# Turning the third batch's probabilities with VectorE and DRAM transfers in a fused cross-attention, convolution and expert kernel

## The reference, cut to what matters

```python
# x (128, 32, 1024), ctx (128, 257, 256); 32 heads of 32, 8 key groups, 4 heads each
scores = einsum('bsgrd,btgd->bgrst', layernorm(x), ctx) / sqrt(32) + mask
x = x + einsum('bgrst,btgd->bsgrd', softmax(scores), ctx)      # cross-attention
x = x + (fft-convolution of layernorm(x) with an S4 kernel + D*u)
z = layernorm(x) @ A.T                                         # 64 experts, rank 8
x = x + ((z * gate) @ B.T) * 2.0                               # gate: softmax over top 16
```

## Time and profile before

| | |
|---|---|
| median of 3 runs | 1288.2 us (1287.83 to 1289.85) |
| the profiled execution | 1290.52 us, span 1288.6 us, mean granted clock 0.992 |
| PE busy | 1232.9 us, 96% of the span |
| ACT, DVE, POOL busy | 1122.9, 959.7, 825.4 us |
| DMA | 166.38 MB, mean 129 GB/s |

### The profile page before, as it was taken

The page is one execution under the profiler, slowest core; times in us unless marked ns, Lnnn a source line. Parts: engine busy times, 40 slices in busy tenths (PEclk is TensorE's granted clock), DMA queues, the critical chain, the costliest instruction groups (busy, mean ns, idle before and its releaser), DMA issues.

```text
span 1288.6 us, 41515 instructions
## 1 busy us (share of the span) xinstructions
PE 1232.9 (96%) x13676; PEld 1083.1 (84%) x13676; DVE 959.7 (74%) x3424; ACT 1122.9 (87%) x3337; POOL 825.4 (64%) x1259
## 2 busy tenths in 40 slices
PE   3679999999999999999999999999999999999997
PEld 2558888888888888888888888888888888888886
DVE  6977777777777777877777777677777877877753
ACT  5889999998999999999999999989999999999841
POOL 4447676776667677666767766676777666777520
PEclk9979999999999999999999999999999999999999
DMA  7443443443344444434544433453443344444210
GB/s 237 134 127 93 151 155 122 130 133 125 119 148 152 124 130 132 129 123 141 155 122 131 147 124 118 134 154 123 131 151 123 122 128 154 132 125 132 61 60 33
DMA packets 150103, 166.38 MB, mean 129 GB/s; under 512 B 58217, under 2 KB 116082, under 8 KB 149890
## 3 DMA queue, kind: packets, MB, share of 16 engines
q1 hardware_dynamic: 149890, 163.72, 40.9%
HBM read 128.50 MB, written 34.08 MB: 126 GB/s over the span
## 4 chain that ended last, share of the span: by engine, by line
PE 76%; DVE 5%; DMA 4%; POOL 4%; ACT 4%; issue 3%; SPq 2%; DVEq 0%; ACTq 0%; POOLq 0%
PE ps_p L562 22%; PE ps_p L633 15%; PE ps_p L661 12%; PE ps_p L648 12%; PE ps_p L594 8%; PE ps_s L574 7%; ACT pr L840 2%; DMA dn<-den 2%; DMA xq<-in_x 1%; POOL lastp L1093 1%; DVE ms L1387 1%; SPq L381 1%; ACT pts L772 1%; DMA vl<-in_ctx 1%; POOL lastp L1103 1%
## 5 line engine op out<-in xcount | busy, mean ns | idle before, releaser
L840 ACT ACTIVATE pr<-ms,negmax 128x256 f32<-128x256 f32 x1024 | 512.6, 504 | 17.3 <-DVE negmax L1387 17.3
L1387 DVE CUSTOM_DVE_ANT_0 ms<-ps_s,neg_mask,last 128x256 f32<-128x256 f32 x1024 | 447.0, 473 | 7.1 <-PE ps_s L574 6.2
L772 ACT ACTIVATE pts<-ps_p 128x512 f32<-128x512 f32 x512 | 298.3, 590 | 45.8 <-PE ps_p L562 29.1
L562 PE MATMUL ps_p<-ident,pr 128*128 128x128 f32 x2048 | 296.5, 280 | 10.4 <-ACT pr L840 5.1
L562 PEld LDWEIGHTS ps_p<-ident,pr 128*128 128x128 f32 x2048 | 229.1, 142 | 48.0 <-issue 17.4
L840 ACT ACTIVATION_READ_ACCUMULATOR pr<-ms,negmax 128x1 f32 x1024 | 199.6, 195 | 0.0
L1061 POOL TENSOR_TENSOR kt<-kr,kt 128x512 fp32r<-128x512 f32 x128 | 164.9, 1288 | 24.1 <-ACT kt L772 24.1
L648 PE MATMUL ps_p<-wa_hi,ut_hi 128*128 128x288 f32 x512 | 159.6, 312 | 1.4 <-DVE ut_lo L1203 1.4
L648 PE MATMUL ps_p<-wa_lo,ut_hi 128*128 128x288 f32 x512 | 151.8, 296 | 0.0
L648 PE MATMUL ps_p<-wa_hi,ut_lo 128*128 128x288 f32 x512 | 151.7, 296 | 0.0
L1203 DVE TENSOR_TENSOR ut_lo<-ps_p,ut_hi 128x512 fp32r<-128x512 f32 x128 | 87.7, 690 | 74.8 <-ACT ut_hi L772 74.5
(11 more groups left out here) (139 smaller groups left out, 2584.6 us busy)
## 6 DMA issues: line engine op xcount, KB each, us to landing
cx<-in_ctx SPq DMA_DIRECT2D x128, 256.0 KB, 3.9
kr<-in_keys SPq DMA_DIRECT2D x128, 256.0 KB, 3.0
xq<-in_x SPq DMA_DIRECT2D x32, 512.0 KB, 4.3
turn_q<-xq SPq DMA_DIRECT2D x32, 512.0 KB, 2.9
qx<-turn_q SPq DMA_DIRECT2D x128, 128.0 KB, 2.9
xr<-in_x SPq DMA_DIRECT2D x32, 512.0 KB, 3.9
out_x<-tmp SPq DMA_DIRECT2D x32, 512.0 KB, 3.2
dn<-den SPq DMA_DIRECT2D x512, 2.0 KB, 2.3
```

The lines of the kernel that those rows point to most:

```text
L562: mm = pe.transpose(into[:, j * P:(j + 1) * P], source, ident[:, :])
L772: return act.activation(out, in_, ACT.Copy, scale=scale)
L840: act.activation(pr[:, b % 2, g, :], ms[:, n % MS, :], ACT.Exp, bias=negmax[:, n % MS:n % MS + 1], scale=-1.0, accum_out=den[:, b, g:g + 1 ...
L1387: dve.tensor_tensor_reduce(ms[:, n % MS, :], ps_s[:, g % GPH, g // GPH * SW:(g // GPH + 1) * SW], neg_mask[:, 0:SW], 1.0, last[:, it % 2, ...
```

## The change

`TURNED = (2,)`: batch 2 of every tile no longer has pair chunks 8 to 11 on PE nor their copies on ACT. Instead
- `exp` writes its 8 groups with the 256 keys split in 2 x 4 x 32, so that in each half (4 groups) a run of 128 elements holds 32 keys of four groups;
- `p_turn` (DVE) transposes the 32x32 blocks of a half in place, 128x1024, twice per tile;
- `store_p` (SP) writes a half, 512 KB, to the DRAM tensor `turn_p`, twice per tile;
- `load_p` (SP) reads it back with keys on the partitions: four transfers of 256 KB into the half of `pts` that batches 0 and 2 share. It waits for both stores and for attend 1;
- `attend` 4 and 5 wait for these four transfers and read `pts` with a view whose runs are 32 elements long.

`move_q` now makes four transfers of 128 partitions each, one per batch, and `load_last` one transfer instead of four. `exp` waits per half of `pr`. `PAIRS` becomes 12. All `BANKS` numbers and all lists of calls are new. Cut to its core:

```diff
+TURNED = (2,)
+def paired(m):
+    return sum(k // GPH not in TURNED for k in range(m))
+PAIRS = paired(STEPS // 2)
+        turn_p = nc.dram_tensor("turn_p", [len(TURNED), P, GPH, HALVES, SW], F32, kind="Internal").ap()
+            def store_p(it, k, h):
+                sp.wait_ge(p_turned[k][h], at(it, 1, 1))
+                if at(it, 64, 0) > 0:
+                    sp.wait_ge(p_loaded[k], at(it, 64, 0))
+                sp.dma_start(turn_p[k, :, :, h, :],
+                             pr[:, TURNED[k] % 2, GPH * h:GPH * (h + 1), :]).then_inc(p_stored[k][h], 16)
+            def load_p(it, k):
+                b = TURNED[k]
+                for h in range(HALVES):
+                    sp.wait_ge(p_stored[k][h], at(it, 16, 16))
+                if at(it, 2 * BPT, 2 * b - 2) > 0:
+                    sp.wait_ge(pv_done, at(it, 2 * BPT, 2 * b - 2))
+                own = pts[:, b % 2 * GPH:(b % 2 + 1) * GPH, :]
+                for r in range(REP):
+                    sp.dma_start(own[:, r, :],
+                                 turn_p[k, SEQ * r:SEQ * (r + 1), :, :, :].rearrange("t i h c -> i t (h c)")).then_inc(p_loaded[k], 16)
             def move_q(tile):
...
-                for quad in range(GPH):
-                    sp.dma_start(qx[SEQ * quad:SEQ * (quad + 1), :, :, :, :].rearrange("p b h r d -> p b (h r d)"),
-                                 turn_q.rearrange("b s (q c) -> s b q c", q=GPH)[:, :, quad, :]).then_inc(q_moved, 16)
+                for b in range(BPT):
+                    sp.dma_start(qx[:, b, :, :, :].rearrange("p h r d -> p (h r d)"),
+                                 turn_q[b, :, :].rearrange("s (q c) -> q s c", q=GPH)).then_inc(q_moved, 16)
             def load_last(tile):
...
-                for c in range(BPT):
-                    sp.dma_start(vl[SEQ * c:SEQ * (c + 1), tile % 2, :],
-                                 context[tile * BPT + c:tile * BPT + c + 1, 2 * P, :]
-                                 .broadcast_to([SEQ, CTX_DIM])).then_inc(vl_loaded, 16)
+                sp.dma_start(vl[:, tile % 2, :],
+                             context[tile * BPT:(tile + 1) * BPT, 2 * P, :].unsqueeze(1)
+                             .broadcast_to([BPT, SEQ, CTX_DIM])).then_inc(vl_loaded, 16)
             def attend(it, hh):
...
+                if b in TURNED:
+                    pe.wait_ge(p_loaded[TURNED.index(b)], at(it, 64, 64))
+                else:
+                    pe.wait_ge(pc_done, at(it, PAIRS, paired(2 * hh + 2)))
+                turned = pts[:, b % 2 * GPH:(b % 2 + 1) * GPH, :].rearrange("p r (h j q s) -> p h j q r s", h=HALVES, j=TBLK, q=GPH)
...
+                                       turned[:, h, j, q, :, :] if b in TURNED else
             def exp(it, n):
...
+                if b in TURNED:
+                    out = pr[:, b % 2, g // GPH * GPH:(g // GPH + 1) * GPH, :].rearrange("p g c -> p (g c)").rearrange(
+                        "p (i j g t) -> p g j i t", i=GPH, j=TBLK, g=GPH)[:, g % GPH, :, :, :]
+                    masked = masked.rearrange("p (j i t) -> p j i t", j=TBLK, i=GPH)
+            def p_turn(it, k, h):
+                b = TURNED[k]
+                dve.wait_ge(e_done, at(it, STEPS, GROUPS * b + GPH * (h + 1)))
+                half = pr[:, b % 2, GPH * h:GPH * (h + 1), :].rearrange("p g c -> p (g c)")
+                dve.transpose(half, half).then_inc(p_turned[k][h], 1)
```

More of the change, by code:

```diff
@@ L35 @@
 STEPS = BPT * GROUPS
-PAIRS = STEPS // 2
+TURNED = (2,)
 PW = SW
@@ L67 @@
 BANKS = {
[L68 to L71, removed]
+    "pair": (1, 0, 0, 1, 0, 2, 0, 3, 2, 1, 3, 1, 0, 3, 1, 3,),
+    "out": (0, 2,),
+    "u": (1, 0,),
+    "z": (3, 1,),
     "g": (1,),
-    "y": (2, 3,),
+    "y": (1, 0,),
     "f": (3, 2,),
-    "b": (1, 0,),
+    "b": (1, 2,),
     "o": (3, 2, 3, 1,),
@@ L205, in build @@
         e_done = sem("e_done")
+        p_turned = [[sem(f"p_turned{b}_{h}") for h in range(HALVES)] for b in TURNED]
+        p_stored = [[sem(f"p_stored{b}_{h}") for h in range(HALVES)] for b in TURNED]
+        p_loaded = [sem(f"p_loaded{b}") for b in TURNED]
         pt_done = sem("pt_done")
@@ L442, in iteration @@
             def iteration(it, odd):
-                turn_last(it)
+                if on(it - 1):
+                    store_p(it - 1, 0, 0)
+                    store_p(it - 1, 0, 1)
                 if on(it - 3):
@@ L470, in iteration @@
                     load_keys(it + 1, 3)
[L471 to L475, removed]
@@ L476, in _ @@
-            load_context(0, 1); load_x(2); load_context(1, 0); move_den(0, 1); load_weight(6); load_keys(1, 3)
-            load_weight(7); turn_last(1); move_den(0, 2); load_keys(2, 0); load_residual(0); move_den(0, 3)
-            store_kernel(); load_strip(); load_context(1, 1); load_last(2); store_q(2); move_q(2); load_keys(2, 1)
-            move_den(1, 0); load_keys(2, 2); load_x(3); store_last(2); move_den(1, 1); load_keys(2, 3)
-            load_context(1, 3)
+                    store_last(it + 1)
@@ new lines, in _ @@
+            load_mask(); load_x(0); load_last(0); load_router(); load_s4(); load_wide(); load_weight(0); store_q(0)
+            load_weight(1); load_keys(0, 0); move_q(0); load_x(1); load_keys(0, 1); store_last(0); load_weight(2)
+            load_weight(3); turn_last(0); load_keys(0, 2); clear_kernel(); load_last(1); load_context(0, 2)
+            load_context(0, 0); load_context(0, 3); load_weight(4); load_keys(0, 3); store_q(1); load_keys(1, 0)
+            move_q(1); load_keys(1, 1); load_context(0, 1); load_weight(5); load_x(2); load_weight(6); move_den(0, 0)
@@ new lines, in _ @@
+            store_p(0, 0, 0); move_den(0, 1); store_last(1); move_den(0, 2); store_p(0, 0, 1); turn_last(1)
+            load_keys(1, 2); load_keys(1, 3); load_p(0, 0); move_den(0, 3); load_residual(0); load_keys(2, 0)
+            load_weight(7); load_context(1, 0); store_kernel(); load_keys(2, 1); load_last(2); load_strip()
+            move_den(1, 0); store_q(2); load_context(1, 1); load_keys(2, 2); move_q(2); load_context(1, 3)
+            move_den(1, 1); load_keys(2, 3); load_x(3); store_last(2)
@@ L486, in _ @@
+            move_den(30, 2); load_p(30, 0); move_den(30, 3); load_context(31, 0); store(28); load_context(31, 3)
+            load_context(31, 1); move_den(31, 1); load_context(31, 2); move_den(31, 0); store_p(31, 0, 0)
+            load_residual(31); store_p(31, 0, 1); move_den(31, 2); load_p(31, 0); store(29); move_den(31, 3)
+            store(30); store(31)
             sp.wait_ge(out_stored, 16 * TILES)
@@ new lines, in _ @@
+            pair_chunk(31, 6); expand(29, 0, 0, 4); expand(29, 1, 0, 2); scores(31, 3); u_chunk(30, 0); u_chunk(30, 1)
+            pair_chunk(31, 7); expand(29, 1, 2, 3); expand(29, 1, 3, 4); convolve(30, 0, 0, 4); convolve(30, 1, 0, 1)
+            convolve(30, 1, 1, 8); z_chunk(30, 0, 0); attend(31, 2); z_chunk(30, 1, 0); pair_chunk(31, 12)
+            attend(31, 3); pair_chunk(31, 13); pair_chunk(31, 14); experts(30, 1, 0, 1); experts(30, 1, 1, 3)
+            pair_chunk(31, 15); experts(30, 1, 3, 4); experts(30, 1, 4, 6); attend(31, 4); attend(31, 5)
@@ new lines, in _ @@
+            z_stats(30, 0, 0); z_stats(30, 1, 0); z_stats(30, 2, 0); normalisers(31); route_step(30, 0)
+            route_step(30, 1); route_step(30, 2); route_step(30, 3); route_step(30, 4); route_step(30, 5)
+            route_step(30, 6); route_step(30, 7); route_step(30, 8); out_half(31, 0); route_step(30, 9); gated(30, 1)
+            gated(30, 0); out_half(31, 1); gated_low(30); u_stats(31, 0); u_stats(31, 1); u_stats(31, 2)
+            third_residual(30, 0, 0); u_low(31, 0); u_low(31, 1); second_residual(31, 0, 1); third_residual(30, 1, 0)
```

484 lines of the change are left out of this document (236 added, 248 removed).

## The result

The changed kernel takes 1670.3 us (median of four runs, 1662.3 to 1677.7) where the kernel before takes 1288.0 in the same comparison (1285.3 to 1289.9): a ratio of 1.297, 95% interval 1.290 to 1.303. The forecast was 1507 us with a range of 1300 to 1610. The sign was right and the size was not: +382 us measured, +219 forecast, and the range ended 60 us too low.

The account below looks back on a forecast made before the run. PE was taken to bound the kernel at 37.5 us per tile. The new chain with load_p on four engines gave 44.8, so 30 x 7.3 = 219 us more: 1290.5 + 219 - 2.3 = 1507 us, range 1300 to 1610.

Parts of the forecast that it names:

- The decision that the outermost dimension of the DRAM side sets the number of engines: load_p, move_q and load_last, outermost 4 in DRAM, get four of 16 DMA engines; load_p then takes 14.6 us.
- The missing landing times of the three new forms: Inference from two kpad stores without landing times: outermost counts under 16 leave another kind of completion; no size given.
- The landing of load_p: On four engines load_p takes 14.6 us from first issue to last landing, landing at A + 43.1.
- The small terms: In batch 2: DVE's turns 1.4 us each; strided exponential writes and strided attend reads taken as costing nothing.
- the sum of the new loop: Second half's turn, store, load and attend chain from one iteration to the next, giving a period of 44.8 us.
- 1.7 for the clock: PE's gap of 7 us per tile brings 3.4 us at half clock, losing 1.7 us, mostly inside the chain.
- A: The moment at which PE reaches attend 4 of the previous tile, from which the chain's times are counted.
- Turn's end, forecast A + 22.5: DVE ends the second turn after 19.4 us of PE work, third_residual 1, u_low 1 and the turn itself.
- just where the turn of q stands: move_q on four engines takes 6 us instead of 1.5, landing about A + 19, at q's turn in DVE's order.
- Store to load_p's issue, forecast 6.0: SP issues out, denominators, a context and turn_last, 5.2 us, while stores land; load_p issued from A + 28.5.
- sixteen engines at -51 us: Rival: load_p on sixteen engines lands at A + 34.2, 1.6 us to spare; 1237 us, up to 1262; chance 0.16.
- PE's saving: Sixteen transposes per tile leave PE: 1.7 us per tile, at most 2.0; period 35.8 us if nothing else intervenes.

Follow-up runs that it names:

- 1: The changed kernel with load_p alone rewritten as four transfers of 32 partitions, outermost dimension 32: 1466.0 us, ratio 1.140.
- 2: The changed kernel with load_p as in 1, and move_q and load_last in the forms of the kernel before: 1447.2 us, ratio 1.126.
- 4: The changed kernel with load_p as eight transfers of 64 partitions, outermost dimension 2: 2000.2 us, ratio 1.555.
- 8: The changed kernel, its three narrow transfers kept, with SP's list in the order of 7: 1582.7 us, ratio 1.230.
- 11: The kernel of 9 with DVE's normalisers moved from ahead of route_step 4 to behind route_step 8: 1322.1 us, ratio 1.027.
- 7: The kernel of 2 with SP's list reordered: batch 2's context before the stores, turn_last between stores and load_p, among other moves: 1324.5 us, ratio 1.031.
- 9: The kernel of 7 with q's store ahead of load_last in SP's list, its move ahead of batch 2's keys: 1326.7 us, ratio 1.029.
- 10: The kernel of 9 with batch 3's denominators right behind batch 2's, ahead of the output's store and the residual's load: 1335.6 us, ratio 1.037.
- 6: The changed kernel with SP's list reordered: batch 2's context before the stores, load_p ahead of turn_last and the output, among other moves: 1668.9 us, ratio 1.298.

## Why the prediction was wrong, point by point

**What held.** The decision that the outermost dimension of the DRAM side sets the number of engines: a share of 0.25 in the windows, 1, 2, 4 and 8 of the experiments. The missing landing times of the three new forms came as I read them, though they are no sure mark: the page of the changed kernel has none for turn_last either (last<-turn), whose form did not change and which has one, 1.9 to 4.5 us, in every other run. In all these forms the small count was on the DRAM side; no run has it on the SBUF side alone. With it held the rule of the Trainium skill (DMA: Bandwidth & Descriptors, section "Why a DMA increments its semaphore by 16 and not by 1"): the traces here agree at 4 rows (a share of 0.24 to 0.26), at 2 (0.12 to 0.13) and at 32 (0.92, with the residual's load beside it). The landing of load_p, forecast at 14.6 us after its issue, took 14.2 (816.29 to 830.45). The attend's idle time, DMA into pts ahead of it, was where I put it, 8.2 us for the 7.3.

The small terms held too. DVE's turn, forecast at 1.4 us, takes 1.23 (the group of 128x1024 transposes). The strided write of the exponentials costs nothing: the mean of all 1024, a quarter of them strided, is 505 ns for 504 in the earlier trace rows, and the longest takes 539. Nor does the strided operand of batch 2's attends: in the run of 11 attends 4 and 5 (the first row, strided) take the 1.08 us of the earlier trace rows, as attends 6 and 7 do (the second row, not strided):

```profile
615.90 1.08 PE L634 MATMUL ps_p<-pts,cx 128*32 128x128 f32 x32
...
617.86 1.08 PE L634 MATMUL ps_p<-pts,cx 128*32 128x128 f32 x32
```

**The step that failed** is the sum of the new loop: 22.5 to the end of the turn, 6 to load_p's issue, 14.6 to its landing, 1.7 for the clock, 44.8 in all. The tile above, with A = 780.67, took 49.8:

- Turn's end, forecast A + 22.5 (24.2 with the clock's 1.7): the store was issued at A + 25.8. Attend, scores and attend at half clock take from 780.67 to 786.04, 5.4 us where the earlier trace rows's durations give 2.9: 2.5 us for the clock, not 1.7, and all of it in the chain. Then DVE waited 1.40 us for qx, which I had seen coming ("just where the turn of q stands") and put at nothing. The rest of the way was 0.6 us shorter than forecast, so 1.6 us more in all.
- Store to load_p's issue, forecast 6.0: 9.9 us (806.43 to 816.29). I took each of SP's entries at its usual issue time. But right behind the two stores the output took 1.06 us and not 0.43, the denominators 3.81 and not 2.42 (in the chain the first waits for ACT until 809.57 and the second takes 1.34 us), and turn_last 2.65 and not 1.79 (its first issue takes 1.22 us). That is 2.9 of the 3.9 us more; the rest is the stores' own issues (1.29 us) and gaps. Why single issues grow to 1.1 to 1.3 us behind the stores was not tried.
- Landing: 0.4 us less.

1.6 + 3.9 - 0.4 = 5.1 us more per tile in this tile, 4.6 by the mean period (49.4 against 44.8): 30 x 4.6 = 138 of the 163 us that were missing. The remaining 25 lie almost wholly in the start: the third reciprocal stands at 187.1 us instead of 157.3, 29.8 us later, where the forecast had one tile's 7.3.

Seen from PE the surplus is the same. PE is busy for 782.3 of the 1000 us from 200 to 1200, so 38.6 us of each period of 49.4, where the forecast had 35.8 and 1.7 for the clock; its wait for load_p is 8.2 for 7.3; and the 2.5 us in which it waits for u_low, behind the turn of q, stand nowhere in the forecast. 1.1 + 0.9 + 2.5 = 4.5 us.

The larger error doesn't show in the forecast but in its lower end. I had priced sixteen engines at -51 us, 1237, with 1.6 us to spare, because I put load_p's issue at A + 28.5. It is at A + 36.0 with sixteen engines too, and the load then takes 8.0 us and not 5.7: it lands at A + 44.1 for a forecast of 34.2, 7.5 us of that from the late issue and 2.3 from the load itself. Experiment 2 is that rival, and it took 1447. So the narrow load was one cause of two, and I took it for the only one. The loop through SP's list was the other: 123 us by 2 and 7. With four engines the same order pays 88 us (8). Of the 382 us the width, at the good order, is 258, the order 88 and what no order tried here removed 37; the three sum to 383. The split depends on which is mended first: with the width first it is 223 (2), then 123 for the order (7), and the same 37.

**Where PE's saving went.** Most of it is there. From 200 to 1200 us PE is busy for these shares, first in the kernel before, then in that of 9:

```profile
200.00:1200.00 1000.00, 996.31 (x11287) 878.99 (x11285) 758.91 (x2755) 915.28 (x2746) 686.56 (x1042) 1.00 0.43 133
```

```profile
200.00:1200.00 1000.00, 941.23 (x10656) 818.53 (x10660) 804.07 (x2772) 842.58 (x2583) 670.70 (x1019) 0.99 0.64 185
```

0.996 x 37.4 = 37.3 us of PE per tile before and 0.941 x 38.3 = 36.0 after: 1.3 us less, of the 1.7 forecast. But no order tried here came nearer to 36.0 than 38.3. In 9, from 200 to 1150 us, PE waits 37.5 us for zg, 13.3 for u_low and 4.1 for load_p, in some 25 tiles: 2.2 us each, and 36.0 + 2.2 = 38.2. In 9, 10 and 11 each wait that was shortened was followed by another of like size (q, denominators, residual, POOL's normalisers). In the kernel before, PE was 99.6% busy and such waits ran beside its work; with less work of its own it reaches them. Whether a fully searched order on sixteen engines would reach 36.0 stays open. None of the versions run here beats the kernel before the change; the nearest, 11, is 2.7% above it, and 7, 9 and 11 can't be told apart. What of the 37 us comes from the new orders of the other engines' lists, which all these versions share, was not tried.

## What to carry to other kernels

Count the outermost dimension on both sides of a transfer before merging several into one: from first issue to last landing, four transfers of 32 partitions with 32 outermost rows took 8.0 us, four of 128 partitions with 4 outermost rows 14.2, eight of 64 partitions with 2 outermost rows 24.8. When a round trip through DRAM is put between two steps, walk through the issuing queue's own list between the store and the load, with each entry's waits and not its issue time only. The load can't be issued before the store has landed, so that gap is the place for an entry that another engine will soon wait for. And when an engine at 99.6% is relieved of 1.7 us per tile, ask which waits its work had covered: here six of them (load_p, q, the maxima, the denominators, the residual, the normalisers) took each other's place.

## What was not expected

- Small transfers behind a narrow load wait for all of it (6), and so do large ones: the residual's landing goes from 3.9 us to 13.0 in the changed kernel, with a DMA share of 0.46 overall. That the four engines that carry the load also carry a part of every other transfer would explain it; no view here shows single engines.
- SP is held as well: its issue of the residual's load, which stands right behind load_p in the changed kernel, takes 1740 ns in the median for 466 before (durations in ns: shortest, median, longest):

```profile
L436 SPq DMA_DIRECT2D xr<-in_x x32: 363/466/1396, 77.8 to 1229.8; - x32
```

```profile
L465 SPq DMA_DIRECT2D xr<-in_x x32: 581/1740/2115, 75.2 to 1596.5; - x32
```

- Even on sixteen engines the turned probabilities load at a lower rate than other traffic: in the kernel of 2 the window below, in the midst of load_p and with the residual's load beside it, has a share of 0.92 at 230 GB/s, 250 for a full one, where the earlier trace rows had 353. I had reckoned with 353. Why was not tried.

```profile
804.00:806.00 2.00, 0.43 (x4) 0.42 (x4) 2.00 (x11) 1.58 (x7) 0.43 (x2) 1.00 0.92 230
```

- Moving two entries of SP's list past a third, with no wait and no transfer changed, was worth 89 us of 1413, more than the other edits of order together.
